# A decoder's three cross-attention layers: maxima of a head in one operation, single banks for the transposed scores, transposed pass 12 heads behind

## The chip, the cores and the metric

The kernel runs on one core of one Trainium2 chip. The metric is the device time of one execution in microseconds (us), as the median of several runs. A core has a matrix engine (TensorE, in the rows PE, with its weight loads as PEld), VectorE (DVE), ScalarE (ACT), GpSimd (POOL) and SyncE, which here only issues transfers (SPq). Each engine works through its own queue in order and waits on semaphores. Matrix products land in PSUM, eight banks of 512 f32 columns a partition; the other engines read them there.

## The reference, cut to what matters

The program is a decoder of four blocks on x (8 batches, 256 positions, 128 channels). Three of its twelve layers are the cross-attention of this change, L0x, L1x and L3x: 16 heads of 8 dimensions, 256 queries against 512 keys of a context, in L3x with one mask for all batches.

```python
x = x + _L0_xattn_ref(_layernorm(x, axis=-1), ctx_1024, L0_xattn_w_q, L0_xattn_w_k, L0_xattn_w_v, L0_xattn_w_o)
...
        scores = jnp.einsum('bhqd,bhkd->bhqk', q, k) * scale
        scores = jnp.where(mask == 0, jnp.asarray(-jnp.inf, scores.dtype), scores)
        attn = jax.nn.softmax(scores, axis=-1)
        out = jnp.einsum('bhqk,bhkd->bhqd', attn, v)
        b, h, s, dk = out.shape
        out = out.transpose(0, 2, 1, 3).reshape(b, s, h * dk)
        return out @ Wo.T + bo
```

L0x has no biases and no mask, L1x has biases, L3x has both. The other nine layers are the same before and after.

## The kernel before, in words

One layer goes over 8 batches of 16 heads. q and k are split into three bf16 parts each, stored to DRAM and loaded back as stacks of 125 rows a head (`q_stack`, `k_stack`), so that one bf16 product over those rows gives the scores closely enough. Every head is computed twice. The first pass ("s") has queries on the partitions: two products of 512 columns, one for each 128 queries, of which DVE takes the maximum over the keys (L722; L719 with the mask added in L3x). After eight heads the negated maxima are split into three bf16 parts ("negate", L740 to L749), transposed on PE (L945), copied to `m_rows` by DVE ("m", L702), stored to DRAM (L544) and loaded back as three more rows of `q_stack` (L547). The second pass ("t", called scores in the old code) has keys on the partitions: four products of 256 columns (L998; in L3x each is followed by one that adds the mask, L1005) over the stack with the maxima in it, so that ACT can take exp at once (L861) into `p_ring`, which holds eight heads. For each group of four heads the "values" (L1038, in two halves) sum exp times v into one of two output tiles; ACT copies them out ("outputs", L868), and after four groups come two "norm" transposes (L899) with a division on DVE, the transpose of the heads (L904), the "project" product (L1065) and the "add" to x on DVE (L763, L769 adds the bias).

The order of the work is written out by hand: `order_by_slots` makes a list for one batch of 16 slots, a slot a head, and every engine walks this list and does its own part of each entry. An entry has a batch offset. The passes overlap: t of batch b stands beside s of batch b + 1 and the projections (x, q, k) of batch b + 2. A t unit uses one of two tiles of two banks (`ps_t`), a 512-column s half and everything else that passes through PSUM one of three single banks in turn (`ps_ring`), and the outputs the last bank: 4 + 3 + 1. In the list before, the values' second group waits on PE for the add of the batch before, because both use the same half of the output bank:

```python
                            if g == 1:
                                wait_step(pe, x_done, b, 0)
                            wait_step(pe, o_done, b, g)
```

In L0x and L1x part of the batches run in a hardware loop, in L3x all are written out.

Of the kernel before, what the change touches and what calls it, by code (L numbers as in the profile page):

```python
# [14 lines left out]
P = 128  # L15
B = 8
# [156 lines left out]
def attention(nc, x_sb, const, w, cfg, ahead):  # L173

    H, hd, nkeys = cfg["heads"], cfg["hd"], cfg["nkeys"]
    causal, cross, rope = cfg.get("causal"), cfg.get("cross"), cfg.get("rope")  # L180
    masked, latent = cfg.get("masked"), cfg.get("latent")
    mask_each = cfg.get("mask_each")
    masked = masked or mask_each
    qk_bias, out_bias = cfg.get("qk_bias"), cfg.get("out_bias")
    scale = cfg["scale"]
    nqc = H * hd // P
    hpc = P // hd
    nkc = cfg["kchunks"]
    nkt = nkeys // P
    vcols = cfg["vcols"]  # L190
    small = hd < 32
    gh = 4 if small else hpc
    groups = H // gh
    hpu = 1 if nkeys == KX else 2
    units = H // hpu

    if causal:
        pieces = [(0, 0, 0, S), (S, 1, P, P)]
    else:
        pieces = [(S * t, t, 0, S) for t in range(nkt)]  # L200
    hcols = 2 * BANK // hpu
    used = sum(p[3] for p in pieces)
    last_unit = lambda g: ((g + 1) * gh - 1) // hpu

    with ExitStack() as ctx:
# [33 lines left out]
        sources = ahead.tiles["src"]  # L239

        def source(par):

            return sources[:, par if small else 0, :] if cross else xT[:]

        if small:

            whole = {"q": sb("q_whole", [P, S]), "k": sb("k_whole", [P, nkeys])}
            rest = {"q": sb("q_rest", [P, S]), "k": sb("k_rest", [P, nkeys])}
            parts = {"q": sb("q_parts", [P, 3, S], BF16), "k": sb("k_parts", [P, 3, nkeys], BF16)}


            q_dram = nc.dram_tensor(cfg["name"] + "q_dram", [5, P, S], BF16)
            k_dram = nc.dram_tensor(cfg["name"] + "k_dram", [3, P, nkeys], BF16)
            m_dram = nc.dram_tensor(cfg["name"] + "m_dram", [2, 3, H, S], BF16)
            two_ones = sb("two_ones", [P, 1])
            q_stack = sb("q_stack", [P, 2, H, S], BF16)
            k_stack = sb("k_stack", [P, 2, H, nkeys], BF16)
        else:
            qm = sb("qm", [P, 2, H, S])
            kT = sb("kT", [P, 2, nkc, nkeys])  # L260
# [20 lines left out]
        ready = sem("ready")

        items = [("x", None, "act")]
        if mask_each:
            items += [("some", 0, "act")]
        if latent:
            items += [("lat", 0, "act")]
        if small:
            items += [("q8", 0, "act")]
        else:  # L290
            for c in range(nqc):
                items += [("q", c, "dve" if rope or mask_each else "act")]
        for c in range(nkc):
            items += [("k", c, "dve" if rope else "act")]
        early = len(items) if small else 0
        vblk = max(1, nkt * vcols // BANK)
        for c in range(vblk):
            items += [("v", c, "dve" if qk_bias else "act")]
        first_s = len(items)
        halves = 2 if H > 1 else 1  # L300
        half_of = lambda h: h // (H // halves)
        for h in range(H):
            if hpu == 2:
                items += [("s", (h, None), "dve")]
            else:
                items += [("s", (h, 0), "dve"), ("s", (h, 1), "dve")]
            if (h + 1) % (H // halves) == 0:
                items += [("m", half_of(h), "dve")]
        if small:
            items += [("norm", 0, "dve"), ("norm", 1, "dve"), ("headsT", 0, "act")]  # L310

        later = {"m": 2, "norm": 3, "headsT": 3}
        if small:
            later["v"] = 4
        stage = [0 if n < early else later.get(it[0], 1) for n, it in enumerate(items)]
        full = [sem.step(f"full_{st}_", max(1, stage.count(st))) for st in range(5)]
        took = {(who, st): sem.step(f"{who}_took_{st}_", max(1, sum(i[2] == who and stage[n] == st for n, i in enumerate(items))))
                for who in ("act", "dve") for st in range(5)}

        def item(kind, which=0):  # L320

            return [n for n, i in enumerate(items) if i[0] == kind][which]

        def made(eng, b, n):

            wait_step(eng, full[stage[n]], b, sum(stage[m] == stage[n] for m in range(n + 1)))

        def taken(eng, b, n):

            key = (items[n][2], stage[n])  # L330
            wait_step(eng, took[key], b, sum((items[m][2], stage[m]) == key for m in range(n + 1)))
# [3704 lines left out]
```

## Time and profile before

| what | value |
|---|---|
| median of 3 runs | 2802.39 us (2800.43 to 2806.69) |
| profiled execution, span on the one core | 2873.4 us |
| TensorE's mean granted clock in it | 0.914 |
| busy in it: PE, DVE, ACT, POOL | 82%, 56%, 46%, 26% |
| L0x, L1x, L3x, first to last instruction, about | 308, 311, 346 us |

For the profiled execution no time beside its span is given; it is 2.5% above the median of the timed runs. The busy share of PE is one of modelled, overlapping ends, so 82% does not mean that PE works at its peak for 82% of the time. The three layers that change are a third of the span.

### The profile page before, as it was taken

The numbers are of one execution on the slowest core, as the hardware profiler recorded it, in microseconds if no ns is written. First come the engines' busy times: TensorE is split into PE (matmuls) and PEld (weight loads), VectorE is DVE, ScalarE is ACT, GpSimd is POOL, SyncE is SP. The second block draws the span as 40 slices with busy tenths as digits, with TensorE's granted clock in tenths as the row PEclk, the third lists the DMA queues.
The fourth block names the chain that finished last, engine by engine and source line by source line (L and its number), as shares of the span: only waits on it lengthen the run. The fifth ranks groups of instructions, "written<-read, shape, count | busy, mean of one in ns | idle before, by whom it ended". The sixth has DMA issues, their size and how long they took to land. (4 is left out here: it accounts for less than half of the span.)

```text
span 2873.4 us, 50064 instructions
## 1 busy us (share of the span) xinstructions
PE 2368.7 (82%) x16598; PEld 1519.1 (53%) x16645; DVE 1611.7 (56%) x5026; ACT 1333.5 (46%) x3199; POOL 743.4 (26%) x1017
## 2 busy tenths in 40 slices
PE   6979888778987688853859999867859998899989
PEld 4634444745554244432646666556747775455553
DVE  4757772146666678732036665542347775777730
ACT  3735552135553255544327767321226665355442
POOL 0123212444434222102543332233521112222100
PEclk9979998979998699976779999978979999899999
DMA  2022225120000222230430000253420000322200
GB/s 75 2 75 85 85 67 171 37 73 31 30 31 1 74 85 84 67 94 18 103 67 1 2 1 1 89 96 107 133 68 2 1 2 20 101 70 76 61 18 15
DMA packets 130797, 159.35 MB, mean 55 GB/s; under 512 B 22881, under 2 KB 93034, under 8 KB 129411
## 3 DMA queue, kind: packets, MB, share of 16 engines
q1 hardware_dynamic: 114964, 131.84, 15.8%
q0 software_dynamic: 12976, 23.22, 3.1%
q8 instruction: 130, 2.13, 0.3%
q10 hardware_dynamic: 2624, 1.32, 0.3%
q14 instruction: 103, 0.84, 0.1%
HBM read 119.87 MB, written 37.74 MB: 55 GB/s over the span
## 5 line engine op out<-in xcount | busy, mean ns | idle before, releaser
L719 DVE CUSTOM_DVE_ANT_0 L3x_ps_ring<-L3x_ps_ring,L3x_mask_q 128x512 f32<-128x512 f32 x256 | 173.9, 709 | 62.3 <-PE L3x_ps_ring L968 48.7
L722 DVE TENSOR_REDUCE L0x_mx<-L0x_ps_ring 128x1 f32<-128x512 f32 x256 | 166.4, 686 | 57.2 <-PE L0x_ps_ring L968 56.3
L861 ACT ACTIVATE L3x_p_ring<-L3x_ps_t 128x1024 f32<-128x1024 f32 x128 | 131.0, 1025 | 140.3 <-PE L3x_ps_t L1005 140.2
L722 DVE TENSOR_REDUCE L1x_mx<-L1x_ps_ring 128x1 f32<-128x512 f32 x256 | 165.7, 685 | 45.6 <-PE L1x_ps_ring L968 44.6
L861 ACT ACTIVATE L1x_p_ring<-L1x_ps_t 128x1024 f32<-128x1024 f32 x128 | 130.4, 1025 | 104.4 <-PE L1x_ps_t L998 103.6
L861 ACT ACTIVATE L0x_p_ring<-L0x_ps_t 128x1024 f32<-128x1024 f32 x128 | 130.5, 1026 | 93.8 <-PE L0x_ps_t L998 93.3
L1381 ACT ACTIVATE L2a_probs<-L2a_ps_s,L2a_top 128x256 f32<-128x256 f32 x256 | 117.8, 472 | 79.4 <-DVE L2a_top L1331 79.4
L998 PE MATMUL L3x_ps_t<-L3x_q_stack,L3x_k_stack 128*128 128x256 bf16 x512 | 120.0, 275 | 5.5 <-ACT L3x_p_ring L861 5.4
L1381 ACT ACTIVATE L3a_probs<-L3a_ps_s,L3a_top 128x128 f32<-128x128 f32 (+1 forms) x256 | 104.0, 422 | 39.0 <-DVE L3a_top L1327 36.8
L1005 PE MATMUL L3x_ps_t<-L3x_mask_k,const_ident_bf 128*128 128x256 bf16 x512 | 119.4, 274 | 0.0
L968 PE MATMUL L0x_ps_ring<-L0x_k_stack,L0x_q_stack 125*128 125x512 bf16 x256 | 99.3, 413 | 22.1 <-DVE L0x_mx L722 16.5
L968 PE MATMUL L1x_ps_ring<-L1x_k_stack,L1x_q_stack 125*128 125x512 bf16 x256 | 98.8, 410 | 22.7 <-DVE L1x_mx L722 16.5
L968 PE MATMUL L3x_ps_ring<-L3x_k_stack,L3x_q_stack 125*128 125x512 bf16 x256 | 96.2, 405 | 13.8 <-DVE L3x_mx L719 9.8
L2292 DVE TENSOR_TENSOR L2f_hid<-L2f_gated,L2f_ps 128x256 f32<-128x256 f32 (+1 forms) x93 | 37.7, 419 | 106.0 <-ACT L2f_gated L2353 70.1
L1265 POOL COPY L3a_wide<-L3a_inverse 128x128 f32<-128x128 f32 x128 | 33.8, 293 | 225.6 <-DVE L3a_inverse L1344 225.6
L1327 DVE CUSTOM_DVE_ANT_0 L3a_ps_s<-L3a_ps_s,const_causal_min 128x128 f32<-128x128 f32 (+1 forms) x256 | 83.9, 390 | 11.6 <-PE L3a_ps_s L1460 11.5
L1331 DVE TENSOR_REDUCE L2a_top<-L2a_ps_s 128x2 f32<-128x512 f32 x128 | 82.0, 682 | 13.1 <-PE L2a_ps_s L1460 13.1
L1761 PE MATMUL L1a_ps_p<-const_max_rows,const_ones_bf 128*128 128x512 bf16 x242 | 71.7, 400 | 17.1 <-DVE L1a_w_cs L3269 15.7
L2353 ACT ACTIVATE L2f_gated<-L2f_ps 128x256 f32<-128x256 f32 (+1 forms) x93 | 34.2, 382 | 110.7 <-PE L2f_ps L2415 48.4
L998 PE MATMUL L0x_ps_t<-L0x_q_stack,L0x_k_stack 128*128 128x256 bf16 x512 | 78.7, 277 | 5.6 <-ACT L0x_p_ring L861 5.6
L998 PE MATMUL L1x_ps_t<-L1x_q_stack,L1x_k_stack 128*128 128x256 bf16 x512 | 78.2, 276 | 5.6 <-ACT L1x_p_ring L861 5.6
L1349 DVE TENSOR_TENSOR L2a_oT<-L2a_ps_o,L2a_spread 128x256 f32<-128x256 f32 x64 | 27.1, 423 | 95.8 <-ACT L2a_spread L1398 83.6
(720 smaller groups left out, 6300.2 us busy)
## 6 DMA issues: line engine op xcount, KB each, us to landing
L0x_k_stack<-L0x_k_dram SPq DMA_DIRECT2D x96, 96.0 KB
L1x_k_stack<-L1x_k_dram SPq DMA_DIRECT2D x96, 96.0 KB
L3x_k_stack<-L3x_k_dram SPq DMA_DIRECT2D x96, 96.0 KB
L0f_w<-L0f_in_w SPq DMA_DIRECT2D x32, 256.0 KB
L1a_rk_wide<-L1a_rk_dram SPq DMA_DIRECT2D x8, 1024.0 KB, 4.7
L1f_w<-L1f_in_w SPq DMA_DIRECT2D x32, 256.0 KB
kept_x<-ctxT SPq DMA_DIRECT2D x24, 256.0 KB, 3.5
L0x_q_stack<-L0x_q_dram SPq DMA_DIRECT2D x96, 48.0 KB
```

Source lines behind the costliest of these rows:

```text
L719: dve.tensor_tensor_reduce(bank, bank, mask_q[:, qt, :], 1.0, 2 * MASKED, ALU.add, ALU.max, accum_out=mx[:, qt, h:h + 1]).then_inc(took_se ...
L722: dve.tensor_reduce(mx[:, qt, h:h + 1], bank, AX, ALU.max).then_inc(took_sem(n), 1)
L861: act.activation(pr, pt, ACT.Exp, scale=scale).then_inc(exp_done.sem, 1)
L968: last = pe.matmul(out, queries[:, t * P:(t + 1) * P], keys[:, 0:seen_keys], start=True, stop=small or not masked)
L998: last = pe.matmul(out, keys[:, t * P:(t + 1) * P], queries[:, q0:q0 + nq], start=True, stop=small and not masked)
L1005: last = pe.matmul(out, const["ident_bf"][:], mask_k[:, par if mask_each else 0, t, q0:q0 + nq], start=False, stop=True)
L1327: last = dve.tensor_tensor_reduce(span, span, const["causal_min"][:, S - keys_of(t):S], 1.0, -2 * MASKED, ALU.add, ALU.min, accum_out=top[ ...
L1331: dve.tensor_reduce(top[:, slot, j, :], bank.rearrange("p (t k) -> p t k", t=QT), AX, ALU.min).then_inc(top_done, 1)
L1381: last = act.activation(probs[:, n % P_RING, t, 0:keys_of(t)], ps_s[:, n % s_banks, S * t:S * t + keys_of(t)], ACT.Exp, scale=-1.0, bias=t ...
L1761: pe.matmul(bank, const["ones_bf"][:], wide, start=True, stop=True)
L2292: dve.tensor_tensor(hid[0:rows, n % 2, i, :], gated[0:rows, m % H_RING, :], h_bank(m)[0:rows, TILE:2 * TILE], ALU.mult).then_inc(h_out, 1)
L2353: act.activation(gated[0:rows, m % H_RING, :], h_bank(m)[0:rows, 0:TILE], ACT.Silu).then_inc(gate_out, 1)
```

## The change

The function `attention`, which served several kinds of layer, becomes `attention_cross`, for these three alone, with all batches written out instead of a loop. What it does otherwise:

- s: a head's two products go into a tile of two banks, and where there is no mask DVE takes both maxima in one operation over 1024 columns. There are two such tiles (`ps_s`, S_SLOTS = 2); m, v and norm use them too, in turn with s.
- t: a head is two halves of two products (four with the mask), each in a single bank of three (`ps_t`, T_BANKS = 3) with an exp over 512 columns; x, q, k and the transposed heads use these banks too.
- The list: t of a head stands 12 heads behind its s instead of 16. All other entries have new places.
- norm: both transposes and the division in one piece. negate: four operations instead of five. The add is one operation, and the bias is added earlier by POOL.

Core of the diff (the order, and what each engine does for s, negate, t, values and add):

```diff
+    LAG = 12
...
+    T_BANKS, S_SLOTS = 3, 2
...
+    for kind, k, time, phase in (("ln", 0, -15, 1), ("ln_rest", 0, -15, 3), ("x", 0, -14, 3), ("q", 0, -12, 2), ("k", 0, -11, 2),
+                                 ("split", 0, -11, 3), ("stack", 0, -5, 3), ("stack", 1, -4, 3), ("stack", 2, -3, 3),
+                                 ("stack", 3, -2, 3), ("v", 0, 3, 3), ("negate", 0, 7, 3), ("m", 0, 9, 3),
+                                 ("negate", 1, 15, 3), ("m", 1, 17, 3)):
+        put(kind, k, time, phase)
+    for g in range(GROUPS):
+        ends = LAG + GH * g + GH - 1
+        put("values_first", g, ends + (1 if g == 2 else 2), 3)
+        put("values_second", g, ends + (2 if g == 2 else 3), 2)
+        put("outputs", g, ends + (3 if g == 2 else 4), 1)
+    put("norm", 0, LAG + 22, 2)
+    put("turned", 0, LAG + 24, 2)
+    put("project", 0, LAG + 25, 2)
+    put("add", 0, LAG + 25, 3)
+
+    both = []
+    for s in range(H):
+        u, off = (s - LAG) % H, 1 if s >= LAG else 0
+        both.append(("t", (u, 0), off))
+        both += places.get((s, 1), [])
+        both.append(("t", (u, 1), off))
+        both += places.get((s, 2), [])
+        both.append(("s", s, 1))
+        both += places.get((s, 3), [])
...
-            at_end = {1: [("ln_rest", 0, 2), ("stack", 3, 1), ("values_first", 3, -1)], 2: [("item", item("x"), 2)],
-                      3: [("item", item("v"), 1)], 5: [("split", 0, 2), ("values_first", 0, 0)], 9: [("add", 0, -1)],
-                      10: [("item", item("m", 0), 1)], 11: [("stack", 0, 2)], 12: [("stack", 1, 2)], 13: [("stack", 2, 2), ("values_first", 2, 0)]}
...
+                    if o in t_place and t_place[o] >= T_BANKS:
+                        wait_out(pe, t_users[t_place[o] - T_BANKS])
+                    if o in s_place and s_place[o] >= S_SLOTS:
+                        wait_out(pe, s_users[s_place[o] - S_SLOTS])
...
+                            last = dve.tensor_reduce(mx[:, :, k], s_bank(o), AX, ALU.max)
...
+                        for t in (0, 1):
+                            dst, kt = t_bank(o)[:, t * S:(t + 1) * S], 2 * j + t
+                            last = pe.matmul(dst, k_stack[:, par, u, kt * P:(kt + 1) * P], q_stack[:, par, u, :], start=True, stop=not masked)
...
+                        act.activation(p_ring[:, u % RING, j * BANK:(j + 1) * BANK], t_bank(o), ACT.Exp, scale=scale).then_inc(out["t"].sem, 1)
...
+                            if k == 1:
+                                wait_tally(pe, y_out, b, 0)
+                            wait_tally(pe, o_done, b, k)
...
+                        dve.tensor_tensor(rows, rows, outputs(1).rearrange("p (t k) -> p t k", t=QT), ALU.add).then_inc(y_out.sem, 1)
```

A place (time, phase) means: time in slots counted from the s of the batch's head 0; phase 1 between the two halves of t, phase 2 before s, phase 3 after s. So the first half's maxima are transposed after s of head 9, and t of head 0 stands at the head of slot 12.

First place, PE's queue in L0x from the transposes of the maxima (ps_ring from mparts) of a batch on. Before, in a batch of the middle (ps_ring from the stacks is s, ps_t is t, ps_o are the values):

```order
L945 MATMUL L0x_ps_ring<-const_ident_bf,L0x_mparts 128x128 x2
L998 MATMUL L0x_ps_t<-L0x_q_stack,L0x_k_stack 128x256 x4
L968 MATMUL L0x_ps_ring<-L0x_k_stack,L0x_q_stack 128x512
L1038 MATMUL L0x_ps_o<-L0x_p_ring,L0x_v 32x256 x8
L968 MATMUL L0x_ps_ring<-L0x_k_stack,L0x_q_stack 128x512
L998 MATMUL L0x_ps_t<-L0x_q_stack,L0x_k_stack 128x256 x4
L968 MATMUL L0x_ps_ring<-L0x_k_stack,L0x_q_stack 128x512 x2
```

The t of the head that needs these maxima comes three to four heads after these rows (head 0, at the next slot 0). Now, from the values and s of head 9 before the transposes:

```order
L639 MATMUL L0x_ps_o<-L0x_p_ring,L0x_v 32x256 x8
L604 MATMUL L0x_ps_s<-L0x_k_stack,L0x_q_stack 128x512 x2
L611 MATMUL L0x_ps_s<-const_ident_bf,L0x_mparts 128x128 x2
L623 MATMUL L0x_ps_t<-L0x_q_stack,L0x_k_stack 128x256 x4
L604 MATMUL L0x_ps_s<-L0x_k_stack,L0x_q_stack 128x512 x2
L623 MATMUL L0x_ps_t<-L0x_q_stack,L0x_k_stack 128x256 x4
L604 MATMUL L0x_ps_s<-L0x_k_stack,L0x_q_stack 128x512 x2
L623 MATMUL L0x_ps_t<-L0x_q_stack,L0x_k_stack 128x256 x4
```

The last row is the t of head 0, which needs what the third row begins: two t and two s stand between, and no values.

Second place, PE's queue in L0x around the project product (from headsT) and the values of the second group. Before:

```order
L1065 MATMUL L0x_ps_o<-kept_x,L0x_headsT 128x128 x2
L968 MATMUL L0x_ps_ring<-L0x_k_stack,L0x_q_stack 128x512
L998 MATMUL L0x_ps_t<-L0x_q_stack,L0x_k_stack 128x256 x4
L968 MATMUL L0x_ps_ring<-L0x_k_stack,L0x_q_stack 128x512
L1038 MATMUL L0x_ps_o<-L0x_p_ring,L0x_v 32x256 x8
```

Now:

```order
L590 MATMUL L0x_ps_t<-kept_x 128x512
L663 MATMUL L0x_ps_o<-kept_x,L0x_headsT 128x128 x2
L604 MATMUL L0x_ps_s<-L0x_k_stack,L0x_q_stack 128x512 x2
L639 MATMUL L0x_ps_o<-L0x_p_ring,L0x_v 32x256 x8
L623 MATMUL L0x_ps_t<-L0x_q_stack,L0x_k_stack 128x256 x4
```

The values that wait for the add have moved to directly behind the s after project; a t and an s half that stood between are gone. On DVE the add (x_sb from ps_o) of a batch now stands between these, behind the maxima of the s that was issued after project:

```order
L485 TENSOR_TENSOR L0x_heads_out<-L0x_ps_s,L0x_inverse 128x128 x2
L444 TENSOR_REDUCE L0x_mx<-L0x_ps_s 128x2 x4
L495 TENSOR_TENSOR x_sb<-x_sb,L0x_ps_o 128x256
L444 TENSOR_REDUCE L0x_mx<-L0x_ps_s 128x2 x2
L454 TENSOR_SCALAR L0x_mparts<-L0x_mx 128x2x8
```

Before, a batch's add was two operations there, with four one-bank maxima ahead and two behind it.

## Rows read from the trace of the kernel before

**Rows 1.** Busy time by stretch: L0x start, five batches, end; L1x, L3x five batches.

```profile
core 0: us, PE busy (x) PEld busy (x) DVE busy (x) ACT busy (x) POOL busy (x), PEclk, DMA share, GB/s
177.10:203.60 26.50, 19.86 (x48) 6.29 (x49) 22.81 (x44) 1.96 (x4) 7.65 (x9) 0.63 0.28 85
237.10:399.00 161.90, 145.24 (x1280) 77.78 (x1281) 125.75 (x291) 95.58 (x126) 38.09 (x45) 1.00 0.30 88
430.20:461.90 31.70, 23.51 (x254) 13.57 (x254) 4.65 (x19) 18.09 (x24) 0.00 (x0) 0.96 0.01 2
1027.60:1192.20 164.60, 145.28 (x1280) 77.99 (x1281) 131.81 (x321) 94.38 (x121) 38.08 (x45) 1.00 0.29 86
2513.10:2699.90 186.80, 174.59 (x1601) 110.43 (x1602) 142.16 (x481) 95.42 (x121) 38.14 (x45) 1.00 0.27 76
```

**Rows 2.** Timeline of L0x, a steady batch: start us, us, engine, line, operation.

```profile
311.07 0.59 PE L915 MATMUL L0x_ps_ring<-L0x_xT,kept_x 128*128 128x256 f32 x2
311.51 0.38 PE L968 MATMUL L0x_ps_ring<-L0x_k_stack,L0x_q_stack 125*128 125x512 bf16 x1
311.73 0.60 PE L998 MATMUL L0x_ps_t<-L0x_q_stack,L0x_k_stack 128*128 128x256 bf16 x4
312.16 0.38 PE L968 MATMUL L0x_ps_ring<-L0x_k_stack,L0x_q_stack 125*128 125x512 bf16 x1
312.62 1.12 PE L925 MATMUL L0x_ps_ring<-kept_x 128*128 128x512 f32 x2
313.58 0.38 PE L968 MATMUL L0x_ps_ring<-L0x_k_stack,L0x_q_stack 125*128 125x512 bf16 x1
313.89 1.07 PE L1038 MATMUL L0x_ps_o<-L0x_p_ring,L0x_v 128*32 128x256 f32 x16
314.00 0.69 DVE L722 TENSOR_REDUCE L0x_mx<-L0x_ps_ring 128x1 f32<-128x512 f32 x1 [0.72 <-PE L0x_ps_ring L968]
314.89 0.61 PE L998 MATMUL L0x_ps_t<-L0x_q_stack,L0x_k_stack 128*128 128x256 bf16 x4
```

**Rows 3.** Timeline of L0x: negate, maxima, add and what waited for them.

```profile
320.43 0.17 DVE L740 TENSOR_SCALAR L0x_mparts<-L0x_mx 128x16 bf16<-128x16 f32 x1
321.37 2.53 DVE L722 TENSOR_REDUCE L0x_mx<-L0x_ps_ring 128x1 f32<-128x512 f32 x4
322.12 0.39 PE L968 MATMUL L0x_ps_ring<-L0x_k_stack,L0x_q_stack 125*128 125x512 bf16 x1 [0.93 <-DVE L0x_mx L722]
323.82 0.47 DVE L763 TENSOR_TENSOR x_sb<-x_sb,L0x_ps_o 128x128 f32 x2
324.35 1.07 PE L1038 MATMUL L0x_ps_o<-L0x_p_ring,L0x_v 128*32 128x256 f32 x16 [0.52 <-DVE x_sb L763]
```

**Rows 4.** Timeline: the maxima's way into the stack, in L0x's first and last batch.

```profile
198.68 0.28 DVE L702 COPY L0x_m_rows<-L0x_ps_ring 128x256 bf16<-128x256 bf16 x1
198.99 0.32 SPq L544 DMA_DIRECT2D L0x_m_dram<-L0x_m_rows  x1
200.41 0.26 SPq L547 DMA_DIRECT2D L0x_q_stack<-L0x_m_dram  x1
...
434.77 0.31 SPq L544 DMA_DIRECT2D L0x_m_dram<-L0x_m_rows  x1
436.58 0.23 SPq L547 DMA_DIRECT2D L0x_q_stack<-L0x_m_dram  x1
```

**Rows 5.** Groups by line and shape: count, busy us, mean ns, idle before.

```profile
L861 ACT ACTIVATE L0x_p_ring<-L0x_ps_t 128x1024 f32<-128x1024 f32 x128 | 130.5, 1026 | 93.8 <-PE L0x_ps_t L998 93.3
L836 ACT ACTIVATE L0x_k_whole<-L0x_ps_ring 128x512 f32<-128x512 f32 x8 | 4.8, 597 | 5.3 <-PE L0x_ps_ring L925 5.3
L939 PE MATMUL L0x_ps_ring<-kept_x 128*128 128x128 f32 x64 | 10.2, 307 | 1.5 <-DVE L0x_mx L722 1.2
L2868 DVE TENSOR_REDUCE L1f_tok_small<-L1f_by_token 128x16 f32<-128x256 f32 x6 | 2.5, 420 | 2.1 <-DVE L1f_by_token L2884 1.9 <-DVE L1f_by_token L2862 0.2
```

**Rows 6.** Timeline of L3x, DVE: maxima with the mask, back to back.

```profile
2610.61 0.14 DVE L719 DVE_READ_ACCUMULATOR2_ANT L3x_mx<- 128x1 f32 x1
2610.61 0.73 DVE L719 CUSTOM_DVE_ANT_0 L3x_ps_ring<-L3x_ps_ring,L3x_mask_q 128x512 f32<-128x512 f32 x1
2611.26 0.73 DVE L719 CUSTOM_DVE_ANT_0 L3x_ps_ring<-L3x_ps_ring,L3x_mask_q 128x512 f32<-128x512 f32 x1
```

More of the change, by code:

```diff
@@ L170, in plan_fidelity, with attention_cross, put @@
         a.take("tail_" + n, shape, loaded=False)
[L173 to L184, printed above, removed]
-    scale = cfg["scale"]
[L186 to L203, printed above, removed]
+def attention_cross(nc, x_sb, const, w, cfg, ahead):
+    H, HD, KT = 16, 8, KX // P
+    qk_bias, out_bias, masked = cfg.get("qk_bias"), cfg.get("out_bias"), cfg.get("masked")
+    scale = cfg["scale"]
+    GH = 4
+    GROUPS = H // GH
+    HALF = H // 2
+    T_BANKS, S_SLOTS = 3, 2
+    places = {}
+    def put(kind, k, time, phase):
+        places.setdefault((time % H, phase), []).append((kind, k, 1 - time // H))
+    for kind, k, time, phase in (("ln", 0, -15, 1), ("ln_rest", 0, -15, 3), ("x", 0, -14, 3), ("q", 0, -12, 2), ("k", 0, -11, 2),
[21 more added lines that the diff above has]
+        both += places.get((s, 3), [])
+    order = [(kind, k, seq + off) for seq in range(-2, B + 2) for kind, k, off in both if 0 <= seq + off < B]
+    t_users = [o for o in order if o[0] in ("t", "x", "q", "k", "turned")]
+    s_users = [o for o in order if o[0] in ("s", "m", "v", "norm")]
+    t_place = {o: n for n, o in enumerate(t_users)}
+    s_place = {o: n for n, o in enumerate(s_users)}
+    assert len(order) == len(set(order))
@@ L238, in attention @@
         xT = sb("xT", [P, S])
[L239 to L260, printed above, removed]
@@ L281, in attention @@
[L281 to L295, printed above, removed]
@@ L296, in attention @@
[L296 to L331, printed above, removed]
-        def took_sem(n):
-            return took[items[n][2], stage[n]].sem
-        src_loaded = sem.step("src_loaded", 16)
@@ L459, in previous @@
[L459 to L489 removed]
+        oT = sb("oT", [P, GROUPS, S])
@@ new lines, in _ @@
+                    if kind == "v" and qk_bias:
+                        wait_full(dve, o)
+                        if b >= 2:
+                            wait_tally(dve, pv_done, b - 1, 0)
+                        for t in range(KT):
+                            last = dve.tensor_tensor(v[:, par, t, :, 0:HD],
+                                                     s_bank(o)[:, 0, t * P:(t + 1) * P].rearrange("p (h d) -> p h d", h=H),
+                                                     b_v[:].rearrange("p (h d) -> p h d", h=H), ALU.add)
+                        last.then_inc(out["v"].sem, 1)
@@ L870, in _ @@
-                passes(act, step)
+                    if kind == "x":
+                        wait_full(act, o)
+                        act.activation(xT[:], t_bank(o)[:, 0:S], ACT.Copy).then_inc(out["x"].sem, 1)
+                    if kind == "q":
+                        wait_full(act, o)
+                        wait_tally(act, q_split, b, 0)
+                        if b == 0:
+                            ahead.loaded(act)
+                        if qk_bias:
+                            act.activation(whole["q"][:], t_bank(o)[:, 0:S], ACT.Identity, bias=b_q[:]).then_inc(out["q"].sem, 1)
+                        else:
+                            act.activation(whole["q"][:], t_bank(o)[:, 0:S], ACT.Copy).then_inc(out["q"].sem, 1)
@@ L1071, in step @@
                         last.then_inc(y_full.sem, 1)
-                passes(pe, step)
         sem.clear()
```

868 lines of the change are left out of this document (264 added, 604 removed).

## The prediction

> **What bounds the kernel now.** I began with the windows [rows 1], whose bounds are the starts of head 0's t (L998) of batches, except the first, which begins with s of head 0. The three steady ones are five batches each: 161.9 / 5 = 32.4 us a batch in L0x, 164.6 / 5 = 32.9 in L1x, 186.8 / 5 = 37.4 in L3x. The granted clock is 1.00 there, DVE is busy 78%, ACT 59%, DMA 0.3. No engine is full, so PE's waits must be counted. The timeline gives PE's pace at this clock from one start to the next [rows 2]: q 0.44 (311.07 to 311.51), one s product 0.22, t 0.43, k 0.96 (312.62 to 313.58), one half of a group's values 1.00, and some 0.1 more after an s. A batch is then 16 x (0.44 + 0.43) = 13.9 for the passes, 8 x 1.1 = 8.8 for values, 4.5 for the rest (q, k, v by its row of 64 products [rows 5], and x, norm, heads, project and m, about 2.1 together, an estimate from their widths): 27.2 us. The remaining 5.2 us in L0x are waits. Two of them stand in [rows 3]: s for the maxima (0.93) and the values for the add (0.52); both are PE waiting for DVE, which is working through a queue of maxima. In L3x the mask doubles t, 27.2 + 16 x 0.43 = 34.1, and only 3.3 us are waits. So the order of DVE's queue against PE's sets the end, and PE's content is the floor.
>
> **The maxima.** DVE's one-bank maxima run back to back at (2.53 - 0.69) / 3 = 0.61 us [rows 3] and last 0.69. One over 1024 columns isn't in the trace. From 256 columns (0.420 [rows 5]) to 512 (0.69) a column costs 1.05 ns, so 1024 last about 1.21 and follow at about 1.13, an estimate; bounds are two of today's (1.22) and one with no growth in its fixed part at all (0.61 + 512 x 0.00105 = 1.15, less some overlap: 1.1). DVE saves 0.1 us a head, 1.5 us a batch, and negate's fifth operation 0.17 [rows 3]. Against this stands when it may begin: before, the first half's maximum began while PE wrote the second half; now it waits for both, as 0.42 us passed between the last product's start and DVE's start (313.58 to 314.00 [rows 2]). A tile is thus held 0.43 + 0.42 + 1.21 + 0.05, 2.1 us a head, and there are two. In L3x the masked maxima remain two operations of 0.65 at a pitch and 0.14 for the accumulator's read [rows 6]; nothing is saved.
>
> **ACT.** Sixteen exps of 1.03 become 32 of about 0.60 (the nearest row is a 512-column operation of ACT, 597 ns [rows 5]): 16 x 0.17 = +2.7 us, 21.8 us a batch. Its cover is ACT's idle 40%; with 32 us to a batch it stays under. I take nothing. The three single banks let PE write a half while ACT reads another; a t doesn't wait in my walk.
>
> **The way of m.** Copy 0.28, store 0.03 behind it, load 1.42 behind the store's issue (1.81 in the last batch), all in [rows 4]. The load's landing isn't shown by a row; I take 1.6, bounded by 1.42 and 1.81 of the first transfer. The t of head 0 can start 0.03 + 1.42 + 1.6 + 0.05 = 3.1 us after the end of m's copy. Before, three to four heads with their values stood between (over 4 us), so nothing waited.
> One page speaks against this placing too: the Trainium skill, "DMA: Bandwidth & Descriptors", section "Anatomy of one DMA — SWDGE (gpsimd) path", gives about 2.0 us fixed for a DMA issued by GpSimd. The row's first transfer took 1.42 from SP's queue; by the page's figure the two transfers would take 1.0 us longer together, an estimate, and the sum would be 21 x 1.0 = 21 us more. The sum goes by the row.
>
> **A walk through L0x.** I laid PE's and DVE's new queues beside each other, each unit by the paces above, from the end of s of head 6 as zero. Slot 8: s waits until 1.41 and ends 1.84, values to 2.94. Slot 9: t 3.38, values 4.48, s 4.91, m's transposes 5.03. DVE takes s 9 until 6.2 and then m's copy, 6.25 to 6.53. Slot 10: t 5.47; its s needs the tile of s 9, so it starts at 6.35, a wait of 0.88. Slot 11 ends at 7.67, all it holds. Slot 12 opens with t of head 0, released at 6.53 + 3.1 = 9.63: **a wait of 1.96**. Behind it on PE are everything else of the slot, s of head 12, and so DVE; SP has nothing but these transfers. The second half of the maxima costs less here, since v and values lie between m (slot 1) and its t (slot 4), but its transposes need an s tile: s 0 is in it, whose maxima are behind negate and ln on DVE: wait 1.35. Slot 3: v waits 0.75 for s 2, and s 0.1 more behind norm. Slot 5: the second group's values wait for the add, which now stands behind the maxima of s 5: s ends, +0.42, +1.21, add about 0.4 after its one-piece form, less the 0.3 that PE's queue needs: **1.75** against 0.52. With 0.3 of small ones the waits are 1.96 + 0.88 + 1.35 + 0.75 + 1.75 + 0.5 = 7.2, and a batch 27.2 + 7.2 = **34.4 us** (+2.0). L1x has the same order, with the bias's add moved to POOL: 34.5 (+1.6). L3x gives 0.66, 1.55, 1.1, 0.57 and 1.96 at the same places, as its longer t hides some: 34.1 + 5.7 = 39.8 (+2.4).
>
> **Fill and end.** In L0x's fill [rows 1] PE is granted 0.63 and DVE is busy 22.8 of 26.5: DVE sets it. Four heads fewer ahead of the first t save 4 x 1.22 = 4.9; twelve shorter maxima 1.1; m's way, of which only the two following heads' maxima (2.3 us) hide a part, gives back about 1.7: 4.3 us sooner a layer. The end (31.7 us in L0x [rows 1]) has t and values alone, and stays. Writing the loop out I cost at nothing: L3x is written out already, L0x's loop batches have the period of its others.
>
> **Sum.** Seven periods a layer: 7 x (2.0 + 1.6 + 2.4) = +42.0; fill -3 x 4.3 = -12.9; together +29 on the profiled span of 2873.4, 1.0%. The median was 2802.39, 0.975 of that span, so +28: **2831 us**. What is needed for no change is 12.9 / 21 = 0.6 a batch: I would have to be wrong by 1.4 us of 7.2 in each batch.
>
> **Rivals.** *The wait for m is hidden* (0.13): if landing is quicker, or PE reaches slot 12 later than I think, 1.96 and 1.55 vanish: 32.4, 32.5 and 38.3 us, 7 x (0 - 0.4 + 0.9) - 12.9 = -9, **2793 us**. For it: SP's queue is otherwise empty; against it: the transfers' 1.42 and 1.81.
> *Two whole tiles free PE from DVE* (0.22, the other side): DVE has 24 us of work for a batch, so if its queue absorbs every delay, only m's wait and the add's old 0.52 remain: 2.5 us a batch, 29.6, 29.7 and 36.6, 7 x -6.8 - 12.9 = -61, **2743 us**. It decides once waits for DVE in L0x fall under 3.3 us (5.9 less m's 1.96, with the fill's gain). For it: PE's floor of 27.2 allows it, and the waits of [rows 3] are of the single ring that everything shared. Against it: a tile is held 2.1 us where the two heads written meanwhile need 1.7.
> *The clock falls in the thin slots* (0.15): the fill shows 0.63 where PE waits between products [rows 1], that is partly 1.2 GHz. Between slots 9 and 12 PE works 1.8 of 4.6 us. At 1.2 GHz what follows takes up to twice as long until it rises: by doubling 1 to 1.7 us of products a batch, 21 to 36 us more, **2851 to 2866 us**. Against it: steady rows with single waits near 1 us show 1.00.
> The Trainium skill, "TensorE: Matmul & The Clock Gate", section "Part 1: The HAM clock gate (the "warmup" mystery)", says that an idle TensorE is gated to 1.2 GHz and must work to come back to 2.4; by it each batch could fall once. The steady windows of before, at 1.00 with 5 us of waits, neither show nor exclude it for a wait twice as long.
>
> **Chances.** My forecast has 0.50; its own range is 2812 to 2850, by 1.1 to 1.22 for the maxima and 1.42 to 1.81 for landing (0.5 us a batch each way, 10 us), and as much for the walk. The case "two whole tiles" is faster, "hidden" half faster and half within 0.2% (5.6 us, about what a measurement tells from no change), the clock slower: faster 0.29, same 0.08, slower 0.63. The range, 2750 to 2868, takes in the clock's case and the faster side down to its middle, leaving out about 0.1 on each side.
>
> **What the profile after would show.** Head 0's t at 34.4, 34.5 and 39.8 us from batch to batch; PE idle about 2 us before it, ended by the load of the stack from DRAM; 1.75 before the second group's values, ended by the add; about 1 before m's transposes, by DVE; maxima of 1.21 us, exps of 0.60, clock 1.00. I am wrong if maxima come much cheaper, if that t starts without a wait, or if the clock is under 1 in steady batches.

## The result, and the profile after

| | median, us | ratio to the kernel before, 95% interval |
|---|---|---|
| before (same chip) | 2804.0 | |
| changed | 2844.86 (2838.02 to 2851.65) | 1.0154 [1.0136, 1.0171] |
| predicted | 2831 (2750 to 2868) | 1.010 |

Slower by 41 us where 28 were forecast. The profiled execution's span is 2845.0 us, as long as its timed runs. The windows of the changed kernel, cut as in [rows 1]: five batches of L0x, L1x and L3x from a t of head 0 to another, and then two single batches of L0x:

```profile
core 0: us, PE busy (x) PEld busy (x) DVE busy (x) ACT busy (x) POOL busy (x), PEclk, DMA share, GB/s
228.30:409.20 180.90, 146.79 (x1281) 75.76 (x1282) 114.94 (x190) 100.23 (x205) 38.16 (x45) 0.98 0.29 79
1031.60:1212.10 180.50, 148.69 (x1281) 76.16 (x1282) 119.45 (x210) 98.58 (x200) 41.36 (x50) 0.97 0.27 79
2469.10:2669.40 200.30, 174.36 (x1601) 109.01 (x1602) 132.23 (x451) 100.40 (x200) 41.38 (x50) 1.00 0.25 72
...
300.40:337.90 37.50, 30.43 (x256) 15.45 (x257) 23.05 (x38) 20.18 (x41) 7.63 (x9) 0.95 0.26 76
337.90:373.80 35.90, 28.86 (x256) 14.90 (x257) 22.95 (x38) 20.07 (x41) 7.64 (x9) 1.00 0.30 81
```

A batch takes 180.9 / 5 = 36.2 us in L0x (before 32.4), 36.1 in L1x (32.9) and 40.1 in L3x (37.4). DVE has less to do, 23.0 us a batch in L0x against 25.2, and PE hardly more. What grew is the time in which PE stands. The list of PE's waits in L0x's five batches (us in total, times, longest):

```profile
PE L0x_ps_t L623 <- DMA L0x_q_stack<-L0x_m_dram: 13.1, 8, 2.1
PE L0x_ps_o L639 <- issue: 8.4, 5, 1.7
PE L0x_ps_s L611 <- DVE L0x_mx L444: 6.8, 5, 1.4
PE L0x_ps_s L604 <- DVE L0x_mx L444: 3.8, 5, 0.8
PE L0x_ps_s L594 <- DVE L0x_mx L444: 2.6, 5, 0.5
```

The list also counts a wait that ends on a bound of the stretch. Its first row holds six waits before t of head 0 and two before t of head 8; the five batches themselves have five and two, 11.2 us together.

Two places of the timeline, the add and the values behind it first, then slots 9 to 12, with all engines mixed:

```profile
358.44 0.60 PE L604 MATMUL L0x_ps_s<-L0x_k_stack,L0x_q_stack 125*128 125x512 bf16 x2
359.07 1.23 DVE L444 TENSOR_REDUCE L0x_mx<-L0x_ps_s 128x2 f32<-128x1024 f32 x1 [0.95 <-PE L0x_ps_s L604]
360.21 0.41 DVE L495 TENSOR_TENSOR x_sb<-x_sb,L0x_ps_o 128x256 f32<-128x256 f32 x1
360.73 1.07 PE L639 MATMUL L0x_ps_o<-L0x_p_ring,L0x_v 128*32 128x256 f32 x16 [1.69 <-issue]
...
368.93 1.23 DVE L444 TENSOR_REDUCE L0x_mx<-L0x_ps_s 128x2 f32<-128x1024 f32 x1 [0.80 <-PE L0x_ps_s L604]
370.07 0.28 DVE L466 COPY L0x_m_rows<-L0x_ps_s 128x256 bf16<-128x256 bf16 x1
370.21 0.60 PE L604 MATMUL L0x_ps_s<-L0x_k_stack,L0x_q_stack 125*128 125x512 bf16 x2 [0.77 <-DVE L0x_mx L444]
370.38 0.32 SPq L349 DMA_DIRECT2D L0x_m_dram<-L0x_m_rows  x1
371.80 0.26 SPq L351 DMA_DIRECT2D L0x_q_stack<-L0x_m_dram  x1
373.83 0.60 PE L623 MATMUL L0x_ps_t<-L0x_q_stack,L0x_k_stack 128*128 128x256 bf16 x4 [2.14 <-DMA L0x_q_stack<-L0x_m_dram]
```

The reader should read two stories here. The first group: the 1.69 us are put down to "issue", but the values start 0.11 us after the add's end (360.21 + 0.41 = 360.62), and the add stood in DVE's queue behind 1.23 us of maxima; it is the wait for the add. The second: DVE's copy of the maxima is also behind such an operation, the load is issued 1.42 us after the store as in [rows 4], what waits for it starts 2.0 us after its issue (371.80 to 373.83), and t of head 0 is released 373.83 - 370.35 = 3.5 us after the copy's end.

### The profile page after: what moved, and what is told of

The parts are those of the page before. It is cut to its first block and busy times, and to the rows that moved or that the text cites. A ratio compares the mean times of both kernels' runs of the same rounds, so it can differ in the third digit from the quotient of the medians.

```text
span 2845.0 us, 48521 instructions
## 1 busy us (share of the span) xinstructions
PE 2345.1 (82%) x16645; PEld 1499.5 (53%) x16645; DVE 1558.6 (55%) x4642; ACT 1358.3 (48%) x3583; POOL 752.7 (26%) x1030
## 5 line engine op out<-in xcount | busy, mean ns | idle before, releaser
L441 DVE CUSTOM_DVE_ANT_0 L3x_ps_s<-L3x_ps_s,L3x_mask_q 128x512 f32<-128x512 f32 x256 | 170.6, 716 | 95.7 <-PE L3x_ps_s L604 95.3
L550 ACT ACTIVATE L3x_p_ring<-L3x_ps_t 128x512 f32<-128x512 f32 x256 | 141.6, 597 | 146.9 <-PE L3x_ps_t L625 146.4
L444 DVE TENSOR_REDUCE L0x_mx<-L0x_ps_s 128x2 f32<-128x1024 f32 x128 | 153.1, 1221 | 97.5 <-PE L0x_ps_s L604 97.2
L444 DVE TENSOR_REDUCE L1x_mx<-L1x_ps_s 128x2 f32<-128x1024 f32 x128 | 153.1, 1221 | 87.2 <-PE L1x_ps_s L604 86.7
L550 ACT ACTIVATE L1x_p_ring<-L1x_ps_t 128x512 f32<-128x512 f32 x256 | 139.5, 604 | 118.5 <-PE L1x_ps_t L623 118.2
L550 ACT ACTIVATE L0x_p_ring<-L0x_ps_t 128x512 f32<-128x512 f32 x256 | 139.5, 604 | 112.5 <-PE L0x_ps_t L623 111.8
L623 PE MATMUL L3x_ps_t<-L3x_q_stack,L3x_k_stack 128*128 128x256 bf16 x512 | 120.3, 275 | 12.3 <-DMA L3x_q_stack<-L3x_m_dram 12.2
L972 ACT ACTIVATE L3a_probs<-L3a_ps_s,L3a_top 128x128 f32<-128x128 f32 (+1 forms) x256 | 104.2, 422 | 38.2 <-DVE L3a_top L918 36.1
L623 PE MATMUL L0x_ps_t<-L0x_q_stack,L0x_k_stack 128*128 128x256 bf16 x512 | 82.3, 282 | 19.3 <-DMA L0x_q_stack<-L0x_m_dram 16.4
L623 PE MATMUL L1x_ps_t<-L1x_q_stack,L1x_k_stack 128*128 128x256 bf16 x512 | 82.7, 283 | 17.0 <-DMA L1x_q_stack<-L1x_m_dram 15.3
L604 PE MATMUL L0x_ps_s<-L0x_k_stack,L0x_q_stack 125*128 125x512 bf16 x256 | 83.1, 411 | 14.2 <-DVE L0x_mx L444 8.6
L604 PE MATMUL L1x_ps_s<-L1x_k_stack,L1x_q_stack 125*128 125x512 bf16 x256 | 82.9, 409 | 14.0 <-DVE L1x_mx L444 8.4
L604 PE MATMUL L3x_ps_s<-L3x_k_stack,L3x_q_stack 125*128 125x512 bf16 x256 | 79.8, 396 | 13.3 <-DVE L3x_mx L441 7.7
L639 PE MATMUL L1x_ps_o<-L1x_p_ring,L1x_v 128*32 128x256 f32 x1024 | 69.2, 389 | 12.4 <-issue 10.1
```

What stands on the lines that cost most here:

```text
L441: last = dve.tensor_tensor_reduce(span, span, mask_q[:, t, :], 1.0, 2 * MASKED, ALU.add, ALU.max, accum_out=mx[:, t, k:k + 1])
L444: last = dve.tensor_reduce(mx[:, :, k], s_bank(o), AX, ALU.max)
L550: act.activation(p_ring[:, u % RING, j * BANK:(j + 1) * BANK], t_bank(o), ACT.Exp, scale=scale).then_inc(out["t"].sem, 1)
L604: last = pe.matmul(s_bank(o)[:, t, :], q_stack[0:MAX_ROW, par, k, t * P:(t + 1) * P], k_stack[0:MAX_ROW, par, k, :], start=True, stop=True)
L623: last = pe.matmul(dst, k_stack[:, par, u, kt * P:(kt + 1) * P], q_stack[:, par, u, :], start=True, stop=not masked)
L639: last = pe.matmul(outputs(k)[32 * j:32 * j + 32, :], v[:, par, t, h, :], p_ring[:, h % RING, t * S:(t + 1) * S], start=(t == 0), stop=(t ...
```

## The experiments

All are the changed kernel with the edit shown, except x0 and x7, which are on the kernel before. Ratios are to the kernel before on the same chip; the changed kernel's is 1.0154.

**x0: the kernel before again.** Its first profiled execution took 2873.4 us where the timed ones took 2802.

> The kernel before, unchanged, for a second trace of it: its first profiled execution took 2.5 per cent longer than the median. If that excess lies outside the three layers of the change, their periods stay at 32.4, 32.9 and 37.4 us and the other layers are some 60 us shorter than in the first trace; if it lies in them, the periods are shorter and the change cost more there than the two traces show.

Span 2797.4 us. The same five batches of L0x, L1x and L3x in this trace:

```profile
232.11:394.05 161.94, 145.13 (x1280) 77.87 (x1281) 125.77 (x291) 95.53 (x126) 38.16 (x45) 1.00 0.31 88
1016.22:1180.82 164.60, 145.31 (x1280) 78.00 (x1281) 131.78 (x321) 94.44 (x121) 38.14 (x45) 1.00 0.30 86
2436.51:2623.27 186.76, 174.56 (x1600) 110.44 (x1601) 142.14 (x481) 95.46 (x121) 38.19 (x45) 1.00 0.25 76
```

They match [rows 1] to 0.1 us. The first trace's excess of 76 us lay outside the three layers, so the periods and fills compared here are the kernel's own.

**x1: the add ahead of the maxima.**

```diff
-    put("add", 0, LAG + 25, 3)
+    put("add", 0, LAG + 25, 2)
```

> Only the add's place changes: from behind the maxima of slot 5 to ahead of them on VectorE. My theory: the 1.7 us that TensorE waits before the second group's values falls to about 0.3, a batch gets 1.3 us shorter, 21 batches 27 us: ratio to the kernel before about 1.005 (the changed kernel has 1.015). Rival: VectorE's queue as a whole sets the pace, so the wait turns up again at the next maxima and the ratio stays at 1.013 to 1.016.

1.0038 [1.0024, 1.0052], 2813.91 us. The wait for the add is gone from the list of L0x's waits, and the others stand about as they were (all six of the first row are before t of head 0, five of them in the five batches):

```profile
PE L0x_ps_t L623 <- DMA L0x_q_stack<-L0x_m_dram: 12.3, 6, 2.5
PE L0x_ps_s L611 <- DVE L0x_mx L444: 6.8, 5, 1.4
PE L0x_ps_s L604 <- DVE L0x_mx L444: 3.9, 5, 0.8
PE L0x_ps_s L594 <- DVE L0x_mx L444: 2.6, 5, 0.5
```

A batch gets 1.4 us shorter in L0x (34.8), 1.8 in L1x (34.3) and 1.6 in L3x (38.4). The rival, one shared limit on VectorE, would have shown the 1.7 us at another row.

**x2 and x11: m's transposes ahead of s.** x2 moves both halves, as in the diff; x11 moves the first alone, with the second left at (17, 3).

```diff
-                                 ("stack", 3, -2, 3), ("v", 0, 3, 3), ("negate", 0, 7, 3), ("m", 0, 9, 3),
-                                 ("negate", 1, 15, 3), ("m", 1, 17, 3)):
+                                 ("stack", 3, -2, 3), ("v", 0, 3, 3), ("negate", 0, 7, 3), ("m", 0, 9, 2),
+                                 ("negate", 1, 15, 3), ("m", 1, 17, 2)):
```

> The two transposes of the maxima stand ahead of s of their slot (9 and 17) instead of behind it, so the copy to m_rows comes before the maxima of that s. My theory: the copy comes 1.2 to 1.5 us earlier, the wait for the stack before t of head 0 falls from 2.0 us to about 0.5 and the one before t of head 8 (0.5) goes; s of slot 10 no longer waits for the maxima of slot 9 (0.8). About 2.2 us a batch in L0x and L1x, 1.5 in L3x: 41 us, ratio 1.000. With no wait of 2 us the granted clock of L0x's and L1x's steady batches is 1.00 instead of 0.97. Rival (the transfers are late whatever the copy does, or VectorE sets the pace): ratio over 1.010.

> Only the first half's transposes stand ahead of s (slot 9), the second half's stay behind s of slot 17. The two together took 0.0157. By the rows of the changed kernel 1.2 us of the wait before t of head 0 and 0.8 us before s of slot 10 belong to the first, 0.5 us before t of head 8 to the second: of the 0.0157 some 0.011 are the first half's, ratio 1.004. Rival (the second half's move, with its wait of 1.4 us for maxima, gave most): 1.010.

x2 0.9997 [0.9983, 1.0011]; x11 0.9962 [0.9950, 0.9974]. The total of x2 came out as expected, but not its parts: x11 was expected at 1.004, and the first half alone gives 0.019, more than both. In x11 the waits for the stack in L0x's five batches are five before t of head 0, 0.6 to 1.5 us and 5.6 in total, instead of 11.2 before both heads; the 0.8 before s of slot 10 is gone; and the granted clock is 1.00, where x2 shows 0.99 in L0x and L1x (one batch of each five at 0.95):

```profile
224.44:393.21 168.77, 143.52 (x1281) 74.57 (x1282) 115.12 (x191) 99.28 (x205) 38.09 (x45) 1.00 0.31 85
```

The second half's move does harm, 0.4 us in a batch at full clock (33.7 us in x2, 33.2 in x11): ahead of s the transposes wait for negate (0.7 us) and s of the next head then for the maxima of s 0 (0.9), where behind s there was one wait of 1.4:

```profile
PE L0x_ps_s L604 <- DVE L0x_mx L444: 4.5, 5, 0.9
...
PE L0x_ps_s L611 <- DVE L0x_mparts L461: 3.5, 5, 0.7
```

**x3 and x5: lag 13 and lag 16.** The one number LAG; everything placed from it (values, outputs, norm, project) moves along.

> t stands 13 heads behind s instead of 12, the transfers of m have one slot more. My theory: the waits before t of head 0 and head 8 shrink by 0.9 and 0.5 us, 1.2 to 1.4 us a batch, 21 batches, less 1.2 us a layer for the longer fill: ratio 1.006. The lag places values and outputs too, so other waits may move by up to 1 us a batch either way (0.999 to 1.014). Rival (lag isn't the cause): 1.015 or more.

> t stands 16 heads behind s again, all else as in the changed kernel. My theory: the waits for the stack go (2.4 us a batch), the fill of each layer gets 4.8 us longer, and as 16 and 12 differ by a group of four heads the values keep the same slots, so that the other waits stay; but project and add fall into slot 9 beside m, where the values wait 0.3 us longer for the add. 21 x -2.1 + 14 = -30 us: ratio 1.005. With the miss of lag 13 in mind, what I fear is two waits beside each other and the clock at 1.2 GHz behind them, 2 us a batch: then 1.020.

x3 1.0169 [1.0150, 1.0188]: a miss, outside the span given and where the rival stood. x5 1.0029 [1.0014, 1.0043]: a little better than expected. In x3 no wait for the stack is left in the five batches of L0x (2.2 us a batch in the changed kernel), yet a batch takes 37.5 us instead of 36.2: m's transposes wait 13.1 us for maxima instead of 6.8, s 6.4 instead of 3.8, 1.8 us a batch together, and PE, at the lower clock, is busy 30.8 us a batch instead of 29.4. The windows of one of its batches in L1x:

```profile
1154.00:1161.00 7.00, 6.92 (x63) 2.93 (x60) 5.41 (x7) 5.11 (x12) 0.00 (x0) 1.00 0.58 181
1161.00:1165.00 4.00, 1.35 (x10) 0.54 (x8) 3.85 (x13) 2.08 (x5) 0.71 (x1) 1.00 0.59 165
1165.00:1168.80 3.80, 3.80 (x28) 1.48 (x30) 1.58 (x3) 0.78 (x2) 0.64 (x1) 0.55 0.05 11
```

With lag 13 the values' places move by a slot and no longer separate m's second transposes from s: two waits on VectorE come together (1161 to 1165, PE busy 1.35 of 4.0 us), and behind them TensorE is granted 0.55, nearly all of it at 1.2 GHz, for 3.8 us. The values there take 1.94 us instead of 1.07. Each of the five batches of L0x and of L1x shows a mean clock of 0.95, three of the five of L3x 0.96. In x3 everything placed from LAG has moved, so that it is the two waits in a row that bring the clock down is read from this place and from x8 and x4 below, not tested alone. With lag 16, which keeps the values' slots, some batches show it too (L0x 33.4 us without, 34.8 with).

**x4 and x8: both moves with lag 12 and with lag 16** (the add as in x1, both halves of m as in x2).

> The add ahead of the maxima of its slot and the transposes of the maxima ahead of s of slots 9 and 17, together. If the two waits are independent places of a batch, as my theory says, the gains add: 1.0154 - 0.0116 - 0.0157 = 0.988, some 33 us under the kernel before. Rival (one shared limit, VectorE's queue, gave both gains): no better than 0.996.

> Lag 16 together with the add ahead of the maxima of its slot and the transposes of the maxima ahead of s. With lag 16 the waits for the stack are gone, but 1.4 us for the add and 2 us (twice 1) before m's transposes stood in each batch. If they are places of their own, they go here too: 34.0 - 1.2 - 1.2 us a batch, ratio 1.0029 - 0.010 - 0.010 = 0.983 (0.979 to 0.989). Rival (VectorE's queue limits by now): 0.995 or more.

x4 0.9924 [0.9897, 0.9952], 2779.22 us; x8 0.9982 [0.9968, 0.9996]. Both beat the kernel before, x4 by 0.8%, but not by what adding foretold (0.988 and 0.983): in x4 the two moves give 0.023 where 0.027 were due, in x8 0.005 where 0.020 were, so x8 came out in its rival's range. But VectorE isn't full there: it is busy 114.4 of 167.6 us in L0x's five batches. In x8 m's two waits in a row show what happened, with the values behind them at half speed:

```profile
1017.84 0.27 PE L611 MATMUL L1x_ps_s<-const_ident_bf,L1x_mparts 128*128 128x128 bf16 x2 [0.85 <-DVE L1x_mparts L461]
1019.00 0.60 PE L604 MATMUL L1x_ps_s<-L1x_k_stack,L1x_q_stack 125*128 125x512 bf16 x2 [0.90 <-DVE L1x_mx L444]
1019.54 1.21 PE L639 MATMUL L1x_ps_o<-L1x_p_ring,L1x_v 128*32 128x256 f32 x16
1020.68 1.03 PE L623 MATMUL L1x_ps_t<-L1x_q_stack,L1x_k_stack 128*128 128x256 bf16 x4
1021.64 1.94 PE L639 MATMUL L1x_ps_o<-L1x_p_ring,L1x_v 128*32 128x256 f32 x16
```

Against x5, the wait for the add (7.1 us in L0x's five batches) is gone in x8 and m's own fell from 9.8 to 7.1, but waits of s for maxima, none of which x5's list has, came to 5.7: 2.8 us a batch instead of 3.6, where my expectation had 2.4 less. So the move of m traded one wait for another, as x2 against x11 shows for its second half. That the add's move gives most of x8's gain follows from these lists; lag 16 with the add's move alone wasn't run. The clock takes back some of it: x8's batches in L0x take 32.6 us or, where it fell (three of five), 34.1. Batches at full clock are 0.8 us shorter than x5's in L0x (33.4) and 1.0 in L3x (36.8 against 37.8).

In x4 the two gains do add, as long as the clock is full. The shorter batches, at 0.99 or 1.00, take 35.4 us in L0x in the changed kernel, 33.8 in x1, 33.7 in x2 and 32.1 in x4, and 35.4 - 1.6 - 1.7 is 32.1; in L1x 35.1, 33.6, 33.4 and 32.0, with 31.9 due. So these two waits are places of their own. What falls short is the clock: five of x4's ten batches in L0x and L1x show 0.95, with PE busy 1.5 us longer. The changed kernel and x1 have five of ten as well, x2 two, so adding had counted on two. Two batches of L0x beside each other:

```profile
258.24:290.35 32.11, 28.80 (x256) 14.93 (x257) 23.06 (x39) 19.90 (x42) 7.62 (x9) 1.00 0.31 90
290.35:324.82 34.47, 30.31 (x256) 15.26 (x257) 23.82 (x39) 19.86 (x41) 7.62 (x9) 0.95 0.30 84
```

Waits for the stack take a part as well, up to 1.8 us before t of head 0 in some of x4's batches and none in others. Where they are long, m's store takes up to 2.3 us until the load is issued, instead of 1.42. That isn't a matter of the distance to k's store ahead of it, which is 2.5 us in both of these batches, nor is it x4's alone (2.3 us in x2 and x11 too):

```profile
284.56 0.36 SPq L344 DMA_DIRECT2D L0x_k_dram<-L0x_k_parts  x1
287.07 0.32 SPq L349 DMA_DIRECT2D L0x_m_dram<-L0x_m_rows  x1
288.49 0.25 SPq L351 DMA_DIRECT2D L0x_q_stack<-L0x_m_dram  x1
...
352.71 0.36 SPq L344 DMA_DIRECT2D L0x_k_dram<-L0x_k_parts  x1
355.22 0.32 SPq L349 DMA_DIRECT2D L0x_m_dram<-L0x_m_rows  x1
357.53 0.25 SPq L351 DMA_DIRECT2D L0x_q_stack<-L0x_m_dram  x1
```

**x6, x9 and x10: the maxima in two operations,** each started when its own product is done; alone, with lag 16 and both moves, with lag 12 and both moves.

```diff
-                            last = dve.tensor_reduce(mx[:, :, k], s_bank(o), AX, ALU.max)
+                            for t in range(QT):
+                                wait_tally(dve, full["s"], b, 2 * k + t + 1)
+                                last = dve.tensor_reduce(mx[:, t, k:k + 1], s_bank(o)[:, t, :], AX, ALU.max)
```

> In the changed kernel TensorE signals each of a head's two s products, and VectorE takes the maxima in two operations of 512 columns (in L3x the two masked ones start apart), the tile of two banks is as before. A 512-column one costs 0.09 us more a head, but the first starts 0.22 us sooner, so a tile is held 0.13 us less in L0x and L1x and 0.22 less in L3x. At five places a batch a wait ends with maxima: -0.6 us a batch and -1.1 in L3x, 16 us: ratio 1.010. Rival (merging the maxima is what VectorE gains from): two operations cost 1.5 us a batch, ratio 1.022.

> x8 with the maxima of a head in two operations, each product signalled by itself. In the changed kernel this took 0.0038 off the ratio; the same waits for a tile of s remain, so 0.979, if they end with maxima as there; 0.985 if VectorE is now the bound and 1.5 us a batch more work on it costs.

> Lag 12, both moves, and the maxima in two operations: 0.9924 - 0.0038 = 0.9886 if independent. The wait for the stack (1.2 to 2.0 us where it occurs) is of transfers and stays.

x6 1.0116 [1.0087, 1.0146] at 2832.56 us; its interval reaches that of the changed kernel (1.0136), so its gain of 0.004 is likely, not shown. x9 0.9968 [0.9955, 0.9981] against x8's 0.9982, x10 0.9914 [0.9885, 0.9944] against x4's 0.9924: within the intervals. For x9 that is a miss, since 0.979 was expected before x8 was known to fall short. What can be said is that going back to two operations costs nothing that shows, though VectorE's busy time in L0x rises from 114.94 to 120.21 us in five batches. Joining them saved work on an engine that had time to spare; the rival's 1.022 is excluded.

**x7: the kernel before with exps by halves and all batches written out.**

```diff
-                        act.activation(pr, pt, ACT.Exp, scale=scale).then_inc(exp_done.sem, 1)
+                            act.activation(p_ring[:, u % RING, 0:BANK], ps_t[:, u % 2, 0:BANK], ACT.Exp, scale=scale)
+                            act.activation(p_ring[:, u % RING, BANK:2 * BANK], ps_t[:, u % 2, BANK:2 * BANK], ACT.Exp, scale=scale).then_inc(exp_done.sem, 1)
...
-            if masked and small:
+            if small:
```

> The kernel before with two things of the change that I took at nothing: each exp of 1024 columns as two of 512 in all three layers, and all batches of L0x and L1x written out. ScalarE gets 2.7 us a batch more work beside an idle 13. My theory: ratio 1.000, at most 1.004, since three short waits of a batch (0.8 us together) end with an exp. Rival (these two made the changed kernel slower): 1.008 or more.

1.0005 [0.9994, 1.0016]: in the kernel before both are free within 0.2%, as taken.

## Why the prediction was right, and where it was off

**The bound and the walk.** Right: PE's waits for VectorE and for the transfers set the period, and each stands where the walk put it. Batches of L0x:

| wait of PE | walk, us | measured, us |
|---|---|---|
| t of head 0, for the stack | 1.96 | 1.88 to 2.14 |
| values of the second group, for the add | 1.75 | 1.69 |
| m's second transposes, for the maxima of s 0 | 1.35 | 1.37 |
| s of slot 10, for the maxima of slot 9 | 0.88 | 0.77 |
| v, for the maxima of s 2 | 0.75 | 0.53 |
| t of head 8, for the stack | 0 | 0.77 and 0.49, in two of five batches |

The two columns don't count alike: the walk lets a product end at its pace (0.44 us for s), the trace at a modelled end (0.60), so that each measured wait is about 0.16 us longer by the walk's count. By that count the batch of 35.9 us waits 8.0 us at these six places, where the walk has 6.7; 0.7 of the difference is t of head 8 and 0.3 t of head 0.

x1 moved one entry of the list and x2 two; alone they took 0.012 and 0.016 off a ratio that was 0.015 too high, and x5, which gives the way of m four more heads, took 0.0125: these waits are shown as the cause. The walk's missing row is the last, where "v and values lie between" did not always hide m's second way: in two batches of five in L0x, in none of five in L1x.

**Unit costs.** The maxima over 1024 columns last 1.22 us (1.21 predicted, though the prediction's own figures, 0.69 + 512 x 1.05 ns, give 1.23), the exps 0.60. The landing, taken at 1.6 behind the load's issue, is 2.0 (371.80 to 373.83), so that the way of m takes 3.5 us instead of 3.1, and the wait before t of head 0 is there 2.3 us by the walk's count instead of 1.96. This is the largest error of a single unit cost. The Trainium skill ("DMA: Bandwidth & Descriptors", "Anatomy of one DMA — SWDGE (gpsimd) path") states about 2.0 us fixed for a DMA from GpSimd. For this load, issued by SP, the rows give the same, for the store 1.42: its figure, given for another path, fits one of the two.

**ACT.** Taken at nothing; its load is (x7). It is busy 20.0 us a batch instead of the 21.8 predicted, as exps in a row overlap in the record (160 of 0.603 us make 87.3 us busy, not 96.5). "A t doesn't wait in my walk" was not quite true: from some t to the next product's start it is 0.6 to 0.7 us instead of 0.44 (344.65 to 345.34 below), perhaps a price of the three single banks, about 0.6 us in this batch by adding three of them up, not tested apart.

```profile
344.21 0.60 PE L604 MATMUL L0x_ps_s<-L0x_k_stack,L0x_q_stack 125*128 125x512 bf16 x2
344.65 0.79 PE L623 MATMUL L0x_ps_t<-L0x_q_stack,L0x_k_stack 128*128 128x256 bf16 x4
345.34 0.60 PE L604 MATMUL L0x_ps_s<-L0x_k_stack,L0x_q_stack 125*128 125x512 bf16 x2
347.32 0.28 PE L611 MATMUL L0x_ps_s<-const_ident_bf,L0x_mparts 128*128 128x128 bf16 x2 [1.37 <-DVE L0x_mx L444]
```

**Periods.** Predicted 34.4, 34.5 and 39.8; measured 35.3 to 35.9 in L0x's batches at full clock, 35.1 in L1x, 40.1 in L3x. In L0x and L1x together five of the ten batches had a low clock: 36.8 and 37.6 us in L0x, three of 36.7 to 36.8 in L1x, 1.4 to 2.2 us more each, about 8 us in all. This was the third rival, held at 0.15 with 1 to 1.7 us in every batch. It came true beside the forecast, in a part of the batches and in two of three layers. The forecast's sum had nothing for it, and its list of what the profile would show has "clock 1.00" and names a clock under 1 in steady batches as a sign of being wrong; with 0.98 and 0.97 that sign was there:

```profile
296.40:300.35 3.95, 1.48 (x8) 0.73 (x9) 2.95 (x4) 1.95 (x5) 0.00 (x0) 1.00 0.10 27
300.35:304.00 3.65, 3.65 (x16) 1.75 (x20) 1.39 (x2) 2.17 (x4) 0.00 (x0) 0.53 0.56 168
```

Behind a stretch with PE busy 1.48 of 3.95 us the chip grants 0.53, nearly all of it 1.2 GHz, and from 304 us on 1.00 again. The Trainium skill ("TensorE: Matmul & The Clock Gate", "Part 1: The HAM clock gate (the "warmup" mystery)") says of an idle TensorE that it falls to 1.2 GHz and comes back to 2.4 by working; the fall and the return in this trace agree, though TensorE was not idle here but at work for 1.48 us of that stretch.

**The sum.** Seven periods a layer: +42 predicted. From the first t to the last head 0's t, L0x, L1x and L3x take 248.4, 247.4 and 275.1 us against 226.6, 228.6 and 258.9 in the first trace of before: +57, 15 more than predicted. About 8 of these are the clock in the ten batches above, and the last period of L0x and of L1x, not among them, is at 0.95 as well, where before it was at 1.00. The rest is the way of m and the halves of t. The fill: s of head 0 to t of head 0 is 23.0, 21.6 and 24.0 against 26.5, 26.8 and 27.8, together -12.5 with -12.9 predicted. The end "stays": it is 1.6 and 0.9 us longer in L0x and L1x and 0.2 shorter in L3x, +2. Sum +47; spans 2845.0 - 2797.4 (x0) = 48, medians 41. So mechanism and fill were right. What the sum lacked is for the larger part the clock, a term that it put at nothing, and for the smaller part the size of the waits. That 2845 still lies in the forecast's own range (2812 to 2850) is luck, since this range was made for other terms than the clock.

Two slips in the prediction's arithmetic, neither of which decides anything: the five waits given for L3x add up to 5.84 us, not 5.7, before any small ones; and 5.9 less m's 1.96 is 3.9, not the 3.3 named as the point where the second rival would begin.

**The other rivals.** "The wait for m is hidden" and "two whole tiles free PE from DVE" are excluded by the waits as they stand. The second may have a true core: with the misplaced entries moved, the same two tiles are faster than the kernel before (x4).

## What to carry to other kernels

When several engines walk one list, lay the two queues beside each other unit by unit and look at what stands ahead of each short operation that somebody waits for: an add and a copy of 0.3 to 0.4 us cost 1.4 to 2 us a batch for standing behind maxima of 1.2 us, and moving a single entry gave 1.2% and 1.9%. Merging two operations makes what stands behind them wait for the whole; here it saved VectorE, which had time to spare, 1.1 us a batch, and undoing it cost nothing. A wait doesn't only cost its own length: in these traces TensorE was at 1.2 GHz for 3 to 4 us behind two waits in a row (x3, x4, x8) or one of 2 us, though not each time. So it is worth trying to keep waits apart with products between them, and a shift of all entries by one slot (lag 13) can bring them together.

## What was unexpected, and what stays open

- No wait in x3's lists is over 1.8 us, and yet its clock is lower (0.95) than that of the changed kernel with waits of 2.1 (0.98). Whether it falls differs between like batches (x8: 32.6 or 34.1 us; x4: 32.1 or 34.5); what decides it isn't settled.
- The time of the maxima's store varies: 1.42 us from store to load in the changed kernel's slot 9, 1.42 to 2.3 in x4, x2 and x11, and 3.1 for the second half in the changed kernel (350.00 to 353.12). What decides it is open; with k's store 2.5 us ahead it took 1.42 in one batch and 2.3 in another. That other transfers then under way cause it is argued, not shown.
- The first half's move alone (x11, 0.9962) together with the add's (x1) wasn't tried. If they add up, it would be 0.9962 - 0.0116 = 0.985; x4 shows that they can add batch by batch and the total still fall short by the clock.
- What the new tiles do by themselves, two of two banks for s and three single banks for t, with the old places of the entries, wasn't run; x6 and x7 test the width of the maxima and of the exps only.
